# Small constants laid beside the identity and loaded in one transfer, an earlier second x, and 4 idle products in place of 12, in a gated cross-attention and routed-FFN kernel

## The reference

```
def lora(x, W, b, A, B): return x @ W.T + b + 2 * ((x @ A.T) @ B.T)     # rank 8
n = layernorm(x)
q, k, v = lora(n, Wq...), lora(ctx, Wk...), lora(ctx, Wv...)            # 16 heads of 16
p = softmax(q * 16**-0.5 @ k.T + bias)                                  # bias: 128 x 16 x 128 x 128
x = x + tanh(g_xattn) * (p @ v)
n = layernorm(x)
e = argmax(n @ Wg + bg)                                                 # one of 8 experts
x = x + tanh(g_ffn) * (gelu(n @ W1[e] + b1[e]) @ W2[e] + b2[e])
```

## Time and profile before

| | us |
|---|---|
| median of 3 runs | 1338.42 (1337.06 to 1340.04) |
| the profiled execution, its own time | 1336.7 |
| its span, first to last instruction | 1334.8 |
| outside the span | 1.9 |
| PE busy | 1290.9 (97%) |
| DVE busy | 1094.4 (82%) |
| POOL busy | 1039.5 (78%) |
| ACT busy | 861.8 (65%) |
| first scores (L466) start | 22.65 |

### The profile page before, as it was taken

The page is one execution under the profiler, slowest core; times in us unless marked ns, Lnnn a source line. Parts: engine busy times, 40 slices in busy tenths (PEclk is TensorE's granted clock), DMA queues, the critical chain, the costliest instruction groups (busy, mean ns, idle before and its releaser), DMA issues.

```text
span 1334.8 us, 42404 instructions
## 1 busy us (share of the span) xinstructions
PE 1290.9 (97%) x12916; PEld 1108.2 (83%) x12916; DVE 1094.4 (82%) x2484; ACT 861.8 (65%) x1912; POOL 1039.5 (78%) x1186
## 2 busy tenths in 40 slices
PE   8999999999999999999999999999996699999997
PEld 6888888888888888888888888888874588888886
DVE  5899999999999999999999999999996355555555
ACT  3777777777777777777777777777774233333332
POOL 4779888988888898889898988889986255454545
PEclk8999999999999999999999999999998799999999
DMA  6556556556555655565555556556640688888884
GB/s 228 195 173 206 180 183 193 188 175 187 198 182 179 187 195 174 181 192 196 179 189 193 175 186 195 188 174 187 197 151 35 206 282 283 284 281 284 284 264 134
DMA packets 111607, 265.03 MB, mean 199 GB/s; under 512 B 16649, under 2 KB 33470, under 8 KB 111424
## 3 DMA queue, kind: packets, MB, share of 16 engines
q1 hardware_dynamic: 98064, 228.88, 54.4%
q0 software_dynamic: 12960, 34.63, 6.7%
q10 hardware_dynamic: 528, 0.84, 0.2%
HBM read 227.17 MB, written 38.94 MB: 199 GB/s over the span
## 4 chain that ended last, share of the span: by engine, by line
PE 66%; DVE 13%; issue 11%; ACT 5%; POOL 2%; DMA 1%; DVEq 1%; SPq 1%; POOLq 0%; ACTq 0%
PE bank L481 11%; PE bank L489 10%; PE bank L628 9%; PE bank L641 9%; PE bank L466 6%; PE bank L519 6%; DVE sc L817 5%; PE bank L571 5%; PE bank L534 3%; ACT PT L691 2%; PE bank L617 2%; PE bank L582 1%; ACT KT L675 1%; PE bank L592 1%; DVE negmax L823 1%
## 5 line engine op out<-in xcount | busy, mean ns | idle before, releaser
L378 POOL TENSOR_TENSOR sc<-sc,negmax 128x1024 f32<-128x1024 f32 x256 | 481.8, 1899 | 35.5 <-DVE negmax L823 31.2
L817 DVE TENSOR_TENSOR sc<-bank,sc 128x512 f32<-128x512 f32 x512 | 328.3, 683 | 21.6 <-PE bank L466 20.6
L823 DVE TENSOR_REDUCE negmax<-sc 128x8 f32<-128x1024 f32 x256 | 312.4, 1220 | 16.9
L691 ACT ACTIVATE PT<-bank 128x512 f32<-128x512 f32 x512 | 278.5, 603 | 0.2
L481 PE MATMUL bank<-cst,sc 128*128 128x128 f32 x2048 | 272.6, 276 | 0.0
L435 POOL DMA_INDIRECT out<-og,ids x142 | 139.8, 984 | 150.1 <-issue 130.9
L481 PEld LDWEIGHTS bank<-cst,sc 128*128 128x128 f32 x2048 | 225.3, 141 | 25.7 <-issue 25.5
L705 ACT COPY OT<-bank 128x512 f32<-128x512 f32 x128 | 75.0, 586 | 151.5 <-PE bank L519 151.5
L421 POOL DMA_INDIRECT rows_dram<-x2n,slot_i x128 | 138.6, 1083 | 29.6 <-issue 26.3
L466 PE MATMUL bank<-KT,QT 32*128 32x256 f32 x2048 | 147.3, 401 | 4.7 <-ACT x2T L727 3.5
L982 DVE SCALAR_TENSOR_TENSOR og<-bank,tg,sc 128x512 f32<-128x512 f32 x71 | 53.3, 751 | 108.0 <-PE bank L641 66.8
(11 more groups left out here) (112 smaller groups left out, 2035.1 us busy)
## 6 DMA issues: line engine op xcount, KB each, us to landing
sc<-in_bias SPq DMA_DIRECT2D x256, 512.0 KB
xg<-rows_dram SPq DMA_DIRECT2D x71, 272.0 KB
w_sb<-in_w SPq DMA_DIRECT2D x71, 257.0 KB
sc<-in_w SPq DMA_DIRECT2D x71, 256.0 KB
x_sb<-in_x SPq DMA_DIRECT2D x128, 128.0 KB, 2.0
CT<-in_ctx_in SPq DMA_DIRECT2D x64, 256.0 KB, 5.4
rows_dram<-vacant SPq DMA_DIRECT2D x9, 272.0 KB, 5.8
out<-og,ids POOLq DMA_INDIRECT x142
```

Source lines behind the costliest of these rows:

```text
L378: nc.gpsimd.tensor_tensor(s, s, m, ALU.add).then_inc(sub_ok, 1)
L691: nc.scalar.activation(PT[:, t.slot(2), 512 * q:512 * q + 512], b_t[q % 2][:], ACT.Exp).then_inc(pt_ready, 1)
L817: nc.vector.tensor_tensor(s, b_s[q][:], s, ALU.add).then_inc(s_used, 1)
L823: nc.vector.tensor_reduce(negmax[:, t.slot(2), 8 * h:8 * h + 8], sc[:, t.slot(4), 1024 * h:1024 * h + 1024].rearrange("p (h k) -> p h k", ...
```

## The change

- Seven small loads go away as loads of their own: the two gates, bq, bk, the gate weights, bg and the row numbers. Their values lie in 38 new columns of `cst`, right behind the identity, and the first load of `cst` takes 166 columns in place of 128. The tiles they had become views into `cst`. The other columns of `cst` keep their values and move up by 38.
- SP issues the second x before the context, and the context after it.
- ACT's tanh, and the routing set-up on DVE, wait for this one load.
- PE runs 4 idle products in place of 12.
- DVE merges the weights and scales the biases ahead of the statistics of the second x.

```diff
-        WARM = 12
+        WARM = 4
...
             load(x_sb[:, 0, :], x_seq[0], x_in[0])
-            load(cst[:, 0:P], consts[:, 0:P], s_id)
-            load(g_raw[:, 0:1], g_xattn.partition_broadcast(P), s_g)
-            load(g_raw[:, 1:2], g_ffn.partition_broadcast(P), s_g)
-            load(CT[:, 0], ctx_in[0], ctx_inn[0])
+            load(cst[:, 0:C_FIRST], consts[:, 0:C_FIRST], s_id)
...
             step(0, FIRST + 1)
-            load(cst[:, P:C_END], consts[:, P:C_END], s_cst)
+            load(CT[:, 0], ctx_in[0], ctx_inn[0])
+            load(cst[:, C_FIRST:C_END], consts[:, C_FIRST:C_END], s_cst)
             load(bv_all[:], bv.partition_broadcast(P), s_b)
-            load(bq_col[:], bq, s_b)
-            load(bk_col[:], bk, s_b)
             for k in range(FIRST + 2, -1):
                 step(0, k)
-            load(wg_sb[:], wg, s_set)
-            load(bg_all[:], bg.partition_broadcast(P), s_set)
-            load(ids8[:], ids_const, s_set)
...
-            act.wait_ge(s_g, 16 * FIRST_DMAS)
-            nc.scalar.activation(tg[:], g_raw[:], ACT.Tanh).then_inc(s_seta, 1)
+            act.wait_ge(s_id, 16)
+            nc.scalar.activation(tg[:], g_raw, ACT.Tanh).then_inc(s_seta, 1)
...
-                dve.wait_ge(s_b, 16 * 3)
+                dve.wait_ge(s_b, 16)
...
-                dve.wait_ge(s_set, 16 * SETUP_DMAS)
+                dve.wait_ge(s_id, 16)
...
             clear()
-            step(0, FIRST + 2)
             merge_weights()
             scale_biases()
+            step(0, FIRST + 2)
```

More of the change, by code:

```diff
@@ L41 @@
 STRIPS = P // STRIP
[L44 to L54, removed]
+C_ID, C_G, C_BQ, C_BK, C_WG, C_BG, C_IDS = 0, 128, 130, 132, 134, 150, 158
+C_FIRST = 166
+C_TRI, C_ONE, C_RUN, C_BASE, C_HALF, C_ODD, C_EVEN, C_PART = 166, 294, 422, 454, 486, 487, 488, 489
+C_TAKE, C_EB, C_JUMP, C_NEXT, C_ROW, C_ACC, C_END = 492, 524, 532, 548, 564, 565, 605
 class At:
@@ L97, in run_steps, with flamingo_block @@
         body(0, s)
-def flamingo_block(nc, x, ctx_in, bias, g_xattn, g_ffn, wqT, bq, aq, bqT, wkT, bk, ak, bkT, wvT, bv, av, bvT,
-                   wg, bg, w1, w2, b2, consts, ids_const, out):
+def flamingo_block(nc, x, ctx_in, bias, wqT, aq, bqT, wkT, ak, bkT, wvT, bv, av, bvT,
+                   w1, w2, b2, consts, out):
     ctx = ExitStack()
@@ L113, in flamingo_block @@
         cst = sb("cst", [P, C_END])
-        ids8 = sb("ids8", [P, 8])
+        ids8 = cst[:, C_IDS:C_IDS + 8]
         vacant = sb("vacant", [P, 2 * ROW])
@@ L125, in flamingo_block @@
         B = {w: sb(f"b{w}", [RANK, HID]) for w in "qkv"}
-        bq_col = sb("bq_col", [P, KC])
-        bk_col = sb("bk_col", [P, KC])
+        bq_col, bk_col = cst[:, C_BQ:C_BQ + KC], cst[:, C_BK:C_BK + KC]
         bk_half = sb("bk_half", [P, 2, KC])
         bv_all = sb("bv_all", [P, HID])
-        bg_all = sb("bg_all", [P, EXPERTS])
-        wg_sb = sb("wg_sb", [P, KC, EXPERTS])
-        g_raw = sb("g_raw", [P, 2])
+        bg_all, g_raw = cst[:, C_BG:C_BG + EXPERTS], cst[:, C_G:C_G + 2]
+        wg_sb = cst[:, C_WG:C_WG + KC * EXPERTS].rearrange("p (c e) -> p c e", c=KC)
         tg = sb("tg", [P, 2])
@@ L206, in flamingo_block @@
         s_w, s_ab = {w: sem(f"s_w{w}") for w in "qkv"}, {w: sem(f"s_ab{w}") for w in "qkv"}
-        s_cst, s_id, s_b, s_g, s_set, s_warm = (sem(t) for t in ("s_cst", "s_id", "s_b", "s_g", "s_set", "s_warm"))
+        s_cst, s_id, s_b, s_warm = (sem(t) for t in ("s_cst", "s_id", "s_b", "s_warm"))
         s_bv, b2_in, b2_ok = sem("s_bv"), sem("b2_in"), sem("b2_ok")
@@ L242, in flamingo_block @@
         og_out = [sem(f"og_out{i}") for i in range(2)]
-        SETUP_DMAS = 3
-        FIRST_DMAS = 2
-        WARM = 12
+        WARM = 4
         SETUP_V, SETUP_W = 2, {"q": 4, "k": 5}
@@ L773, in scale_biases @@
                 nc.vector.tensor_scalar(bv_all[:], bv_all[:], tg[:, 0:1], None, ALU.mult).then_inc(s_bv, 1)
-                nc.vector.tensor_scalar(bq_col[:], bq_col[:], D ** -0.5, None, ALU.mult).then_inc(s_setb, 1)
+                nc.vector.tensor_scalar(bq_col, bq_col, D ** -0.5, None, ALU.mult).then_inc(s_setb, 1)
                 for e in range(2):
-                    nc.vector.tensor_scalar(bk_half[:, e, :], bk_col[:], half_rows[e], None, ALU.mult).then_inc(s_setb, 1)
+                    nc.vector.tensor_scalar(bk_half[:, e, :], bk_col, half_rows[e], None, ALU.mult).then_inc(s_setb, 1)
             def merge_weights():
@@ L804, in set_up_routing @@
                                  ).then_inc(vacant_ok, 1)
-                dve.wait_ge(s_set, 16 * SETUP_DMAS)
+                dve.wait_ge(s_id, 16)
                 dve.wait_ge(s_setr, 3)
                 dve.wait_ge(s_setg, 2)
-                nc.vector.tensor_copy(x2id, ids8[:]).then_inc(s_setr, 1)
+                nc.vector.tensor_copy(x2id, ids8).then_inc(s_setr, 1)
                 dve.wait_ge(s_wg, 1)
-                nc.vector.tensor_copy(wg_pad[:, :, 0:EXPERTS], wg_sb[:]).then_inc(s_wg, 1)
+                nc.vector.tensor_copy(wg_pad[:, :, 0:EXPERTS], wg_sb).then_inc(s_wg, 1)
             def add_bias(t, q):
@@ L896, in step @@
                             dve.wait_ge(best_ok, gate.per(4))
-                        nc.vector.tensor_tensor(L[:], log_ps, bg_all[:].unsqueeze(1).broadcast_to([P, 4, EXPERTS]),
+                        nc.vector.tensor_tensor(L[:], log_ps, bg_all.unsqueeze(1).broadcast_to([P, 4, EXPERTS]),
                                                 ALU.add).then_inc(l_ok, 1)
@@ L1022 @@
         "x": a["x"], "bias": np.ascontiguousarray(a["fside_Bx16xSxS2_0"].transpose(0, 2, 1, 3)).reshape(N, P, HEADS * P),
-        "g_xattn": a["g_xattn"].reshape(1), "g_ffn": a["g_ffn"].reshape(1),
     }
@@ L1030, in strips @@
         return np.ascontiguousarray(m.reshape(-1, HID))
+    cols = {}
     for w in "qkv":
@@ L1035 @@
             wt, b, bt = strips(wt), np.ascontiguousarray(strips(b).reshape(KC, P).T), strips(bt)
-        b = b.reshape(1, HID) if w == "v" else b
-        arrays[f"w{w}T"], arrays[f"b{w}"], arrays[f"b{w}T"] = chunks(wt), b, np.ascontiguousarray(bt)
+        cols[w] = b
+        arrays[f"w{w}T"], arrays[f"b{w}T"] = chunks(wt), np.ascontiguousarray(bt)
         arrays[f"a{w}"] = a[f"L0_xattn_A{w}"]
-    arrays["wg"] = chunks(a["L0_ffn_Wg"])
-    arrays["bg"] = a["L0_ffn_bg"].reshape(1, EXPERTS)
+    arrays["bv"] = cols["v"].reshape(1, HID)
     w1 = np.stack([chunks(m).reshape(P, KC * HID) for m in a["L0_ffn_W1"]])
@@ L1067 @@
     c[:, C_ROW] = np.arange(P) * FT
+    c[:, C_G], c[:, C_G + 1] = a["g_xattn"].reshape(1), a["g_ffn"].reshape(1)
+    c[:, C_BQ:C_BQ + KC], c[:, C_BK:C_BK + KC] = cols["q"], cols["k"]
+    c[:, C_WG:C_WG + KC * EXPERTS] = chunks(a["L0_ffn_Wg"]).reshape(P, KC * EXPERTS)
+    c[:, C_BG:C_BG + EXPERTS] = a["L0_ffn_bg"].reshape(1, EXPERTS)
+    c[:, C_IDS:C_IDS + 8] = np.arange(P)[:, None] + P * np.arange(8)[None, :] - 8 * P
     arrays["consts"] = c
-    arrays["ids_const"] = (np.arange(P)[:, None] + P * np.arange(8)[None, :] - 8 * P).astype(np.float32)
     nc = bacc.Bacc("TRN2", target_bir_lowering=False, num_devices=1)
-    order = ["x", "ctx_in", "bias", "g_xattn", "g_ffn", "wqT", "bq", "aq", "bqT", "wkT", "bk", "ak", "bkT",
-             "wvT", "bv", "av", "bvT", "wg", "bg", "w1", "w2", "b2", "consts", "ids_const"]
+    order = ["x", "ctx_in", "bias", "wqT", "aq", "bqT", "wkT", "ak", "bkT", "wvT", "bv", "av", "bvT", "w1", "w2", "b2",
+             "consts"]
     aps = [nc.dram_tensor(f"in_{n}", arrays[n].shape, mybir.dt.from_np(arrays[n].dtype), kind="ExternalInput").ap()
```

## The result

| | before | changed |
|---|---|---|
| median of 22 runs each, us | 1336.47 (1334.14 to 1340.04) | 1339.49 (1337.98 to 1342.56) |
| ratio | 1 | 1.0021 (95%: 1.0015 to 1.0026) |
| profiled execution: span | 1334.8 | 1338.8 |
| first queries start | 14.76 | 16.89 |
| first scores start | 22.65 | 24.83 |

The changed kernel is about 3 us slower. I had forecast no change, on a base of 1338.42 (the median of three runs; 22 runs give 1336.47). The opening shows 2.1 us of it at the queries and 2.2 at the scores; a single profiled execution differs by another us or two elsewhere, so the medians are what counts.

A forecast was written before the change was run, and what follows sets the result against it. The opening chain through the second x's landing to the first queries was taken as the bound; load gains and later statistics left queries at 14.75 against 14.76, 0.0 us, hence 1338.4 us, 8 in 10 within 1335.8 to 1340.9.

The forecast's parts named there:

- Loads, the first slow stretch: DMA queues in the opening: without the gates, full rate (340 GB/s) from 3.3 us; second x lands near 4.
- Loads, all landed by 7.7: DMA queues: 1.50 MB left to land from 3.3 us, 4.4 us at 340 GB/s, so all landed by about 7.7.
- Tanh: ACT in the opening: tanh waits for the table load until 5.55; tg at 5.8, 2 us earlier, hidden by the next item.
- Idle products: PE's opening: free at 3.8, 12 rank-8 products run cold in 5.5 us, k done at 9.3; gives PE 1.25 us.
- "no landing above is later": PE's rank-8 products: no load lands later than the product needing it, with v done at 5.6, q 7.5, k 9.3.
- DVE's new order: DVE's opening: second x's statistics stand behind wk's merge and the biases, starting at 10.64 against 9.83, 0.8 later.
- the slack of 0.8: PE before the second x's transposes: xn ready at 12.84, transposes at 13.66; the later statistics use this up.
- The sum: First query products: start at 14.75 against 14.76, so 0.0 us; 1338.4 for the median.
- Rival B: DMA queues: slow stretch stays for another reason, factors of k land at 9.64, +2.3 us, 1340.7; chance 0.10.
- Rival A: PE in the opening: it warms up early and the queries run warm, 3.0 us faster, 1335.4; chance 0.15.
- The rule on small descriptors: Gate loads: small pieces cost almost nothing, so the slow stretch has another cause and remains, +2.3 us; set aside.

The follow-up runs named there:

- bv as rows: Changed kernel with bv stored as 128 equal rows, so its load reads 128 different rows: median 1338.38 us, ratio 1.0012 to the kernel before.
- the two with the factors ahead: Changed kernel, statistics first, bv as 128 rows, factors of q and k issued before those weights on ACT's queue: 1334.05 us; also without idle products: 1333.80 us.

## Why the prediction was wrong, step by step

- **Loads, the first slow stretch: right.** 349 GB/s from 3.3 us on. The second x landed at about 5.3, not near 4.
- **Loads, all landed by 7.7: the step that failed.** The weights of k landed at 11.54 in place of 7.7, 3.8 us late, for two reasons. First, the prediction let 1.50 MB flow, the loads up to bv. The queues had moved 2.31 MB by then, 0.8 more, since SP had gone on to issue the next context, two x's and the attention bias from 3.54 on. The rate of 340 GB/s was right (338 with bv as rows), the bytes were short: with bv as rows the weights land at 10.0, after 2.26 MB, so in these two profiles 2.3 us of the 3.8 are bytes that the sum left out. Second, bv was counted as 128 KB like any other. It is the same kind of load as the gates, one place read by all partitions, and makes up the rest. I had seen the pattern, and had blamed only the gates. The kernel before has no second slow stretch (317 GB/s from 6.5 to 8.5 us); that bv's slowness was hidden there in the queue that the gates had backed up is my reading and not shown. The factors of k were late by the same step: forecast at 6.5, they released PE at 8.58.
- **Tanh: right.** It started at 5.56.
- **Idle products: the level was right, the end too early.** The rank-8 products ran cold, as forecast; the price was 0.459 a record, 5.5 for all 12, and measured were 2.07, 2.07 and 2.07, with waits of 0.15 and 0.31 for factors that "no landing above is later" had ruled out. The k products ran from 8.58 to 10.65 and not to 9.3. So even with the weights in time the release of DVE would have been late; in the version with bv as rows the k products give it at 10.37 in place of 9.45. Taking eight away from the kernel before makes no difference (0.9996), and neither does giving eight back to the changed one (1.0020).
- **DVE's new order: the mechanism was right, its release wrong.** The statistics stand behind the merge of wk, "which needs the k products": it needs the weights too, and those came last. Merge at 11.63 in place of 9.45, statistics at 12.83 in place of 10.64. From there the working held: 4.11 us from the statistics to the queries forecast, 4.06 measured. The statistics came 3.0 us later than before (12.83 against 9.83), not 0.8, and the queries that much less the slack of 0.8.
- **The sum:** loads forecast as used up by the order, 0.0. The runs say loads -2.4 us, order +2.9 on the loads of before and +4.4 on the new ones, idle products nothing. These parts don't add up to the +3.0 that was measured, since the order takes away what the loads give: with it, the time is 1.0022 with the loads of before and 1.0020 to 1.0021 with the new ones. The new loads bring the second x 4.4 us forward (9.73 to 5.35), but the merge of wk, behind which the order puts it, only 0.3 (11.93 to 11.63).
- **Luck.** The measured 1339.49 lies inside the stated 1335.8 to 1340.9, but only because the base that the range was set around was 2 us high. The change from the kernel before was forecast as 0.0 and is +3.0.
- **Rival B** had the right place for a loss (DVE's statistics no longer run ahead, and what they wait for lands late) and, by luck, the right size, +2.3 against 2.1 at the queries, since it named the factors of k, landing at 9.64, and a slow stretch from 3.3 us on that stayed. That stretch went; what was late were the weights, behind bv and the bytes that the sum had left out. **Rival A** did not occur: the rank-8 records stayed 0.43 us apart. **The rule on small descriptors** of the Trainium skill (DMA: Bandwidth & Descriptors, Why small descriptors are slow) was set aside for the row of the gates. The traces bear it out in part, in that size alone doesn't explain that row: with pieces as small, but at 128 addresses, the same stretch moves 213 GB/s in place of 69, and a load with 1 KB pieces from one place was slow as well. What is left of the slow stretch, 213 against 349, would go against "almost nothing" if small pieces are its cause, which no run tests by itself.

What stays open: the medians differ by 3.0 us and the openings by 2.2. Whether the rest is the clock's rise was not settled: it comes at another moment in each profile, even in those of one shape (queries of 1.99 to 2.89 us), and each version has one profile only.

## What to carry to other kernels

When a load comes earlier, look at what stands ahead of its first use in the consumer's own program, and not only at the load: here a 0.6 us pair of instructions was put behind a merge that needs other, later data, and the order lost more than the loads gained. Before taking a stall away, list every transfer of the same kind, since the next one of them may only have been hidden by the first. When adding up what the queues must move, count what is issued behind the load as well, since another queue's later loads share the bandwidth: here 0.8 MB more than the 1.50 counted. Value what is moved one part at a time and then together; here the parts were -2.4, +2.9 and 0 us and the whole +3.0, and a combination of the good ones beats both kernels, the one before by about 0.2%.

## What the runs showed of the hardware

- A load whose source is one row read for all 128 partitions slows both queues while it runs. For bv (128 KB) the stretch has 121 to 222 GB/s in four profiles, against 316 to 360 in six with the same bytes from 128 rows; for 4-byte pieces 69 to 74 in three, against 213 in one. The weights of k, on ACT's queue and in the same order there, took 6.8 to 7.7 us to land in the four and 5.5 to 6.2 in four of the six; in the two with the factors ahead they took 6.8 and 7.3.
- With 12 idle products ahead (five profiles) the four records of the q products took 1.02 us, the higher level; with 4 or none (nine profiles) 2.07, the lower. In all five the first values, 3 to 5 us on and behind more 8-row products, took 1.91 to 2.08, the lower level again, and no gain in time is seen (0.9996 without eight of them, 1.0020 with them).
- PE's records had the durations of the lower level through 10 us of PE work without a gap (8 to 18) when 2 us of 8-row products stood in its middle (one profile). With those products at the head the clock rose within the first queries or just ahead of them in all six profiles of that shape (queries of 1.99 to 2.89 us against 3.78).
- The stretches' clock column says 1.00 ahead of the first recorded change, although the distance of the records is that of the lower level (0.427 us for 256 columns). Read the durations there, not the column.
